# Cross-attention on one core: the K projection by seven 64x64 products per 2x2 step in place of eight

## What is computed

```python
Q = x @ W_Q      # x: 1024 x 128, W_Q: 128 x 1024, 16 heads of 64
K = ctx @ W_K    # ctx: 6404 x 128
V = ctx @ W_V
scores = Q K^T / 8                 # per head: 1024 x 6404
attn = softmax(scores, axis=-1)
out = (attn @ V, heads side by side) @ W_O + x
return (out - mean(out)) / sqrt(var(out) + 1e-5)   # per row
```

## Time and profile before

| | |
|---|---|
| median of 3 runs | 1600.99 us |
| the profiled execution | 1601.11 us |
| its span in the trace | 1599.3 us |
| TensorE matmuls busy | 1590.5 us (99%) |
| VectorE busy | 1314.6 us (82%) |
| ScalarE busy | 835.4 us (52%) |
| GpSimd busy | 64.2 us (4%) |
| odd pass, even pass | 91.0 us, 104.0 us |

### The profile page before, as it was taken

How to read it: one execution, slowest core, us unless ns; L and a number is a source line. 1 busy time by engine, 2 the same in 40 slices (tenths; PEclk the granted TensorE clock), 3 DMA queues, 4 the chain that set the end, 5 groups by cost and what they waited for, 6 DMA issues and landing times.

```text
span 1599.3 us, 39500 instructions
## 1 busy us (share of the span) xinstructions
PE 1590.5 (99%) x17484; PEld 1073.0 (67%) x17484; DVE 1314.6 (82%) x1229; ACT 835.4 (52%) x828; POOL 64.2 (4%) x41
## 2 busy tenths in 40 slices
PE   9999999999999999999999999999999999999998
PEld 4576677766777667766677666776677766777435
DVE  7788788887888788887798878988789887888877
ACT  4445554555545555456544565445654455544653
POOL 0001000010000001000010000000000000000100
PEclk9999999999999999999999999999999999999999
DMA  4000000000000000000000000000000000000000
GB/s 162 3 2 9 1 2 9 2 10 1 10 2 1 10 1 10 2 1 9 1 10 2 2 9 2 10 2 2 9 1 10 2 9 2 1 10 2 9 2 15
DMA packets 13006, 14.26 MB, mean 9 GB/s; under 512 B 4784, under 2 KB 8624, under 8 KB 12832
## 3 DMA queue, kind: packets, MB, share of 16 engines
q1 hardware_dynamic: 12544, 11.36, 2.3%
q10 hardware_dynamic: 288, 0.33, 0.1%
HBM read 10.60 MB, written 0.59 MB: 7 GB/s over the span
## 4 chain that ended last, share of the span: by engine, by line
PE 98%; DVE 1%; ACT 0%; issue 0%; DVEq 0%; ACTq 0%
PE o_ps L484 44%; PE s_ps L467 42%; PE w_ps L549 6%; PE w_ps L532 5%; PE s_ps L616 0%; DVE inv_sum L943 0%; DVE y L976 0%; DVE stats L963 0%; PE w_ps L564 0%; DVE y L959 0%; PE w_ps L607 0%; DVE inv_sum L809 0%; DVE sums L835 0%; DVE limits L985 0%; DVE k_all L809 0%
## 5 line engine op out<-in xcount | busy, mean ns | idle before, releaser
L728 ACT ACTIVATE probs<-s_ps 128x1024 f32<-128x1024 f32 x801 | 822.5, 1027 | 737.1 <-PE s_ps L467 737.1
L835 DVE TENSOR_TENSOR sums<-sums,probs 128x1024 f32<-128x1024 f32 x785 | 968.0, 1233 | 213.7 <-ACT probs L728 205.5
L484 PE MATMUL o_ps<-probs,v_all 64*64 64x512 f32 x6408 | 942.9, 589 | 0.0
L467 PE MATMUL s_ps<-q_sb,k_all 64*64 64x512 f32 x6408 | 942.8, 589 | 0.0
L467 PEld LDWEIGHTS s_ps<-q_sb,k_all 64*64 64x64 f32 x6408 | 447.8, 133 | 238.9 <-issue 39.0
L484 PEld LDWEIGHTS o_ps<-probs,v_all 64*64 64x64 f32 x6408 | 424.8, 133 | 204.9 <-issue 33.6
L532 PEld LDWEIGHTS w_ps<-wv_sb,ctx_all 64*64 64x64 f32 x3176 | 122.4, 132 | 30.6 <-issue 1.7
L809 DVE TENSOR_REDUCE k_all<-w_ps 128x512 f32<-128x1024 f32 (+2 forms) x104 | 122.8, 1181 | 16.0 <-PE w_ps L549 14.9
L809 DVE TENSOR_REDUCE v_all<-w_ps 128x512 f32<-128x1024 f32 (+2 forms) x103 | 121.8, 1182 | 15.8 <-PE w_ps L532 15.7
L532 PE MATMUL w_ps<-wv_sb,ctx_all 64*64 64x128 f32 x3176 | 120.0, 269 | 0.1
L549 PE MATMUL w_ps<-ctx_all,wk_sb 64*64 64x512 f32 (+2 forms) x832 | 119.3, 573 | 0.0
(11 more groups left out here) (85 smaller groups left out, 119.5 us busy)
## 6 DMA issues: line engine op xcount, KB each, us to landing
inv_sum<-inv_dram SPq DMA_DIRECT2D x30, 128.0 KB, 2.9
ctx_all<-in_ctxT SPq DMA_DIRECT2D x11, 256.0 KB, 5.1
quad_rows<-quad_sums SPq DMA_DIRECT2D x60, 4.0 KB, 1.8
x_sb<-in_x SPq DMA_DIRECT2D x1, 512.0 KB, 10.1
wo_sb<-in_wo SPq DMA_DIRECT2D x1, 512.0 KB, 11.3
left_rows<-p_left SPq DMA_DIRECT2D x30, 8.0 KB
inv_left<-inv_dram SPq DMA_DIRECT2D x30, 8.0 KB
wq_sb<-in_wq SPq DMA_DIRECT2D x1, 448.0 KB, 6.4
```

Source lines behind the costliest of these rows:

```text
L467: last = nc.tensor.matmul(s_ps[part(half), u % 2, head * QH:(head + 1) * QH], k_all[part(head), c * P + half * DH:c * P + (half + 1) * DH] ...
L484: last = nc.tensor.matmul(o_ps[part(head), rows, :], v_all[part(rows), c, part(head)], probs[part(rows), u % RING, head * QH:(head + 1) * QH],
L728: nc.scalar.activation(probs[:, u % RING, :], s_ps[:, u % 2, :], ACT.Exp, scale=SCALE).then_inc(probs_ready, 1)
L835: nc.vector.tensor_tensor(out=sums[0:rows, t % 2, :], in0=sums[0:rows, t % 2, :], in1=probs[0:rows, u % RING, :], op=ALU.add).then_inc(sum ...
```

## The change

From the second pair on, K of each of the 12 full blocks is made by Strassen's scheme: W_K of the pair is a 2x2 matrix of 64x64 blocks, the context of 256 keys a 2x2 matrix of 64x128 blocks, and seven products of sums and differences of blocks replace eight. A block of 512 keys is two such steps, so 14 matmuls of 128 columns instead of 16 times 128 columns. Four of the seven contract in one row half (`one`) and three in the other (`two`), and `one` alternates with the block's number.

- **TensorE**: the work splits in a first part "r" (`seven_first`, 8 matmuls, two in each quarter) and a second part "k" (`seven_second`, 6 matmuls: two in each quarter of row half `one`, one in each of `two`). r stands at steps 0, 4, 8, ..., k at 2, 6, 10, ... and v at 3, 7, 11, ...; in the odd passes r, k, v stand at 38, 40, 41 and 42, 44, 45.
- **ScalarE** copies three of the products to the other 64 partitions, and one as it is, between r and k (`cross`, three instructions).
- **GpSimd** takes two differences of them (`sum_crossed`, two instructions of 128 columns), and makes the sums and differences of W_K once per pair (`form_weights`, 8 instructions).
- **VectorE** finishes K with three instructions (`take_seven`) where there was one.
- The sums of context blocks (`c_forms`, 128x768 floats a block) don't fit in SBUF. GpSimd makes them once, during the first two passes, a block at a time (`form_keys`, four instructions): SyncE reads the context with its halves exchanged, GpSimd adds, SyncE writes 393 KB to `forms_dram`. Later SyncE reads them back, two slots ahead of r.
- GpSimd's `add_halves` and `norm` of the first pass now stand behind all of `form_keys`, and SyncE's `quad_rows` of the first pass behind all of the writing and behind the first reads.
- The keys of a block lie in `k_all` in another order, which `product` undoes by its choice of V's chunk.

```diff
--- before.py
+++ after.py
+    NEXT_STEPS = (0, 36, 38, 40, 41, 42, 44, 45)
+    NORM_STEP, W_FORMS_STEP = 13, 20
+    LEFT_BEHIND = 7
...
+    def by_seven(pair, b):
+        return pair > 0 and 0 <= b < FULL_BLOCKS
...
+            if by_seven(pair, at // 4 + 2) and at % 4 in (0, 2):
+                return ("rk"[at % 4 // 2], pair, at // 4 + 2)
             if at >= 0 and at % 4 == 0 and at // 4 + 2 < BLOCKS:
                 return ("k", pair, at // 4 + 2)
-            if at >= 2 and at % 4 == 2 and at // 4 + 2 < BLOCKS:
+            if at >= 2 and at % 4 == (2 if t == 0 else 3) and at // 4 + 2 < BLOCKS:
                 return ("v", pair, at // 4 + 2)
-        elif pair + 1 < PAIRS and c in (0, 36, 38, 40, 42, 44):
-            n = (0, 36, 38, 40, 42, 44).index(c)
-            return (("q", "q", "k", "v", "k", "v")[n], pair + 1, (0, 1, 0, 0, 1, 1)[n])
+        elif pair + 1 < PAIRS and c in NEXT_STEPS:
+            n = NEXT_STEPS.index(c)
+            return ("qqrkvrkv"[n], pair + 1, (0, 1, 0, 0, 0, 1, 1, 1)[n])
...
+            READY[found] = READY[before] + (before[0] != "r") if len(COUNT) > 1 else 1
+            before = found
...
+        c_forms = sb("c_forms", [P, 2, FORM_COLS])
+        w_forms = sb("w_forms", [P, 6, 2 * DH])
+        crossed = sb("crossed", [P, BLOCK, P])
+        forms_dram = nc.dram_tensor("forms_dram", [FULL_BLOCKS, P, FORM_COLS], F32, kind="Internal").ap()
...
+            def load_turned(b):
+                if b > 0:
+                    sp.wait_ge(c_forms_ready, b)
+                if b > 1:
+                    sp.wait_ge(c_forms_stored[b % 2], 16 * (b // 2))
+                for half in range(2):
+                    sp.dma_start(crossed[part(half), :, :].rearrange("p n k -> p (n k)"),
+                                 ctxT[part(1 - half), b * BK:(b + 1) * BK]).then_inc(turned_ctx_loaded, 16)
...
+            def store_forms(b):
+                sp.wait_ge(c_forms_ready, b + 1)
+                sp.dma_start(forms_dram[b, :, :], c_forms[:, b % 2, :]).then_inc(c_forms_stored[b % 2], 16)
+            def load_forms(pair, b):
+                n = seven_index(pair, b)
+                if n < 2:
+                    for slot in range(2):
+                        sp.wait_ge(c_forms_stored[slot], 16 * (FULL_BLOCKS // 2))
+                else:
+                    sp.wait_ge(work_done, COUNT["k", pair - (b < 2), (b - 2) % FULL_BLOCKS])
+                sp.dma_start(c_forms[:, n % 2, :], forms_dram[b, :, :]).then_inc(c_forms_loaded[n % 2], 16)
+            def load_turned_w(pair):
+                if pair > 1:
+                    sp.wait_ge(work_done, COUNT["k", pair - 1, FULL_BLOCKS - 1])
+                for half in range(2):
+                    sp.dma_start(w_forms[part(half), 0, :], w_k[part(1 - half), pair * P:(pair + 1) * P]
+                                 ).then_inc(turned_w_loaded, 16)
+            load_turned(0)
+            for b in range(FULL_BLOCKS):
+                if b == LEFT_BEHIND:
+                    load_left(0)
+                store_forms(b)
+                if b + 1 < FULL_BLOCKS:
+                    load_turned(b + 1)
             sp.wait_ge(left_zeroed, 2)
             for t in range(PASSES - 1):
+                pair, h = (t + 1) // 2, (t + 1) % 2
+                if h == 1 and pair + 1 < PAIRS:
+                    load_turned_w(pair + 1)
+                    for b in range(2):
+                        load_forms(pair + 1, b)
+                if h == 0:
+                    for b in range(2, 5):
+                        load_forms(pair, b)
                 sp.wait_ge(quad_sums_ready, t + 1)
                 for i in range(QUADS):
...
+                if h == 0:
+                    load_forms(pair, 5)
                 sp.wait_ge(inv_lines_ready, t + 1)
...
+                if h == 0:
+                    for b in range(6, FULL_BLOCKS):
+                        load_forms(pair, b)
...
+            def form_keys(b):
+                one, two = part(b % 2), part(1 - b % 2)
...
+                nc.gpsimd.tensor_tensor(out=forms[one, :, 0:2, :], in0=as_is[one, :, :, :], in1=turned_ctx[one, :, :, :],
+                                        op=ALU.add).then_inc(c_form_step, 1)
+                pool.wait_ge(c_form_step, 3 * b + 1)
+                nc.gpsimd.tensor_tensor(out=forms[two, :, 0, :], in0=as_is[two, :, 1, :], in1=turned_ctx[two, :, 0, :],
+                                        op=ALU.subtract).then_inc(c_form_step, 1)
+                pool.wait_ge(c_form_step, 3 * b + 2)
+                nc.gpsimd.tensor_tensor(out=forms[two, :, 1, :], in0=as_is[two, :, 0, :], in1=as_is[two, :, 1, :],
+                                        op=ALU.add).then_inc(c_form_step, 1)
+                pool.wait_ge(c_form_step, 3 * b + 3)
+                nc.gpsimd.tensor_tensor(out=forms[two, :, 2, :], in0=turned_ctx[two, :, 0, :], in1=turned_ctx[two, :, 1, :],
+                                        op=ALU.add).then_inc(c_forms_ready, 1)
...
+            def sum_crossed(pair, b):
+                n = seven_index(pair, b)
+                pool.wait_ge(crossed_ready, 3 * (n + 1))
+                m4, m3, m1 = (1, 2, 3) if b % 2 == 0 else (2, 3, 1)
+                nc.gpsimd.tensor_tensor(out=crossed[:, m4, :], in0=crossed[:, m4, :], in1=crossed[:, 0, :],
+                                        op=ALU.subtract).then_inc(crossed_summed, 1)
+                pool.wait_ge(crossed_summed, 2 * n + 1)
+                nc.gpsimd.tensor_tensor(out=crossed[:, 0, :], in0=crossed[:, m3, :], in1=crossed[:, m1, :],
+                                        op=ALU.subtract).then_inc(crossed_summed, 1)
...
+            for b in range(FULL_BLOCKS):
+                form_keys(b)
+            pool.wait_ge(c_forms_ready, FULL_BLOCKS)
+            for t in range(1, PASSES):
+                for c in range(FULL_CHUNKS):
+                    if c == 0:
+                        add_halves(t - 1)
+                    found = work_at(t, c)
+                    if found is not None and found[0] == "r":
+                        sum_crossed(found[1], found[2])
+                    if c == NORM_STEP:
+                        norm(t - 1)
+                    if c == W_FORMS_STEP and t % 2 == 1 and t // 2 + 1 < PAIRS:
+                        form_weights(t // 2 + 1)
...
+            def seven_first(found):
+                _, pair, b = found
+                n, one, two = seven_index(pair, b), b % 2, 1 - b % 2
+                main, extra, m1 = seven_slots(b)
+                pe.wait_ge(work_ready, READY[found] - 1)
+                pe.wait_ge(w_forms_ready, pair)
+                pe.wait_ge(c_forms_loaded[n % 2], 16 * (n // 2 + 1))
+                for i in range(2):
+                    g = part(1 - i)
+                    nc.tensor.matmul(main[g, 0, 1, :], w_form(one, 0, 1 - i), form(one, pair, b, i, 0), start=True, stop=True)
+                    nc.tensor.matmul(extra[g, 0, :], w_form(two, 5, i), form(two, pair, b, i, 2), start=True, stop=True)
+                for i in range(2):
+                    h = part(i)
+                    at = pair * P + i * DH
+                    nc.tensor.matmul(main[h, 1, 1, :], wk_sb[part(one), at:at + DH], form(one, pair, b, i, 1),
+                                     start=True, stop=True)
+                    last = nc.tensor.matmul(m1[h, :], w_form(two, 3, i), form(two, pair, b, i, 0), start=True, stop=True)
+                last.then_inc(work_done, 1)
...
+            def seven_second(found):
+                _, pair, b = found
+                n, one, two = seven_index(pair, b), b % 2, 1 - b % 2
+                main, extra, _ = seven_slots(b)
+                pe.wait_ge(crossed_ready, 3 * (n + 1))
+                for i in range(2):
+                    nc.tensor.matmul(extra[part(i), 1, :], w_form(two, 4, i), form(two, pair, b, i, 1), start=True, stop=True)
+                for i in range(2):
+                    at = b * BK + 2 * i * P
+                    nc.tensor.matmul(main[part(i), 1, 0, :], w_form(one, 1, i), form(one, pair, b, i, 2), start=True, stop=True)
+                    last = nc.tensor.matmul(main[part(1 - i), 0, 0, :], w_form(one, 2, 1 - i), ctx_all[part(one), at:at + P],
+                                            start=True, stop=True)
+                last.then_inc(work_done, 1)
...
+            def cross(pair, b):
+                n = seven_index(pair, b)
+                act.wait_ge(work_done, COUNT["r", pair, b])
...
+                apart = w_ps[:, :, :].rearrange("p r (s k) -> p (r s) k", k=P)[:, 1 + b % 2 * 2:6 + b % 2 * 2:2, :]
+                for half in range(2):
+                    nc.scalar.activation(crossed[part(1 - half), 1:4, :], apart[part(half), :, :],
+                                         ACT.Copy).then_inc(crossed_ready, 1)
+                nc.scalar.activation(crossed[:, 0, :], seven_slots(b)[2], ACT.Copy).then_inc(crossed_ready, 1)
...
+            def take_seven(found):
+                _, pair, b = found
```

(13 more changed lines are left out.)

119 lines of the change are left out of this document (94 added, 25 removed).

## The result

The changed kernel takes 1650.4 us (median of four runs, 1649.6 to 1651.2), the kernel before beside it 1600.8: a ratio of 1.031, with a 95% interval of 1.029 to 1.033. The change costs 49.6 us. The forecast was 1632, its range 1608 to 1658. The direction was right and so was most of the mechanism; the size was 18 us short.

What follows compares the result with a forecast made beforehand. The prediction took TensorE, with a matmul in flight 99% of the span, as the bound. It added 1.3 + 3.9 + 19.5 + 6.2 + 0.3 = 31.2 us to 1601.1 us, giving 1632 us, range 1608 to 1658.

Steps and rivals of the forecast that it cites:

- Rival 1: Rounds of sums at the start much longer, 12.5 us each, giving a 28 us stall and 1654 us; chance 0.12.
- Rival 2: TensorE's small matmuls don't keep up, 2 x 0.11 us a block, 18 us in all, 1650 us; chance 0.07.
- ordinary waits (passes 1.3, V's wait 3.9): TensorE: 84 blocks 0.015 us dearer each without a lead, and V waiting 0.05 us for K in 77 blocks.
- steps 2, 40 and 9: Other VectorE work queued there makes TensorE wait 0.86, 0.83 and 1.1 us, 7 times each, +19.5 us.
- stall in the second pass: `quad_rows` lands at 152.8 behind twelve rounds of sums, so TensorE stalls until 156.2, +6.2 us.
- first pass: GpSimd's hold on the port it shares with VectorE, +0.3 us.
- walk through VectorE's queue: From K's second part: VectorE free at 0.81, `take_seven` ends at 2.15, V starts at 2.20 instead of 2.16.
- ScalarE's three copies ... I cost them at nothing: About 1.3 us a block in the 3.4 us between r and k, costed at nothing.
- upper bound of 0.3 us: Most that V's ordinary wait could be, if `cross` or GpSimd's shared port pushes VectorE's addition back.
- No lead gain: TensorE's lighter quarters could run ahead, gaining at most 8.2 us, but V's wait for K prevents it; none taken.
- rival 4: Matmuls in program order, VectorE just in time: nothing saved, little lost, 1602 to 1612 us; chance 0.08.
- Rival 3: Faster, 1593 us: `take_seven` ends before 1.95 us, the lead survives and the start's sums are hidden; chance 0.08.

Runs made afterwards that it cites:

- e_moves_3: `e_moves_2` with the read of block 5's sums put ahead of the wait for `quad_sums` on SyncE's queue; 1624.1 us, ratio 1.015.
- e_moves: The changed kernel with the once-a-pass steps (turn, folding, inversion, norm, left keys' addition, `add_halves`) moved to other places; 1630.4 us, ratio 1.018.
- e_setup: The changed kernel with the first pass's inverses ahead of the last rounds of sums on SyncE's queue; 1641.0 us, ratio 1.025.
- e_two_copies: The changed kernel without the third of ScalarE's three copies (K wrong in the blocks by seven); 1651.6 us, ratio 1.032.
- e_all_3: The changed kernel with `e_spread`, `e_moves_3` and `e_setup` together, and K of the last keys at step 41 instead of 40 in even passes; 1596.4 us, ratio 0.9971.
- e_short_take: The changed kernel without the last of the three VectorE instructions in K's taking (K wrong in the blocks by seven); 1627.7 us, ratio 1.017.
- e_all: The changed kernel with K's second part and VectorE's takings of K and V earlier, plus `e_moves_2` and `e_setup`; 1619.7 us, ratio 1.012.
- e_moves_2: `e_moves` with the folding at step 8 instead of 5; 1632.4 us, ratio 1.019.
- e_spread: The changed kernel with TensorE's r and V of the blocks by seven each behind the product of their step; 1623.3 us, ratio 1.013.

## Why the prediction was right, and where it was short

The measured time lies in the range, but 4 us outside the forecast's own part of it (1618 to 1646). It fell where the range had been widened for rivals 1 and 2, and what happened was neither of them. So that the range held owes something to luck. The forecast passes were 106.5 and 92.0 us, the measured ones 108.4 and 92.35. The terms of the sum, forecast and measured (us):

| step of the prediction | forecast | measured | shown by |
|---|---|---|---|
| ordinary waits (passes 1.3, V's wait 3.9) | 5.2 | 17.4 (7 x 2.48) | what `e_moves_3` has left over before |
| steps 2, 40 and 9 | 19.5 | 18.9 | `e_moves_3`: 22.5, less the next line |
| step 2, V (not forecast) | 0 | 3.6 (7 x 0.51) | `e_moves` |
| stall in the second pass | 6.2 | 9.0 to 9.3 | `e_setup` |
| first pass | 0.3 | 0.9 | windows |

**The walk through VectorE's queue was right in its parts.** The taking's 1.34 us is exact. The three once-a-pass waits, 0.86, 0.83 and 1.1 forecast, are 0.76 (`r` at step 4), 0.95 (`r` at step 42) and 1.04 (V at step 11). That they don't hang on hundredths was right too: all of them vanish when the steps are moved, and come back elsewhere when they are put too close.

**The ordinary wait was mis-sized, and it turned out to be nearly the largest term.** The step that failed is "ScalarE's three copies ... I cost them at nothing". The forecast had it in its upper bound of 0.3 us. They end 0.1 us too late, and the exponential, the addition and the taking shift by 0.08, which `e_two_copies` shows (a block of 8.72 in place of 8.80, and this exponential 1.19 us behind its scores in place of 1.27). What is left to 0.20 is near the forecast 0.065, plus 0.05 us by which `r` comes later behind V (2.64 us, 2.59 where V doesn't wait, as in `e_all_3`). Such a small number stands 84 times in the sum; a wait that is worked out as the difference of 2.20 and 2.16 can't be known to better than 0.1. It could shrink by 0.05 at most and grow by 0.25, so its likeliest value should have lain further from the lower bound.

**The wait at step 2 was missed.** The prediction gave GpSimd's port a price in the first pass alone, and named it besides only in the upper bound of the ordinary wait. The even passes had `add_halves` before too, but beside a taking from PSUM, which it didn't disturb. The diff moves nothing on GpSimd's queue ahead of `add_halves`; it is VectorE's order beside it that changed, and I read VectorE's queue only against TensorE.

**The stall was 3 us short.** A round takes 10.77 us, not 10.5 ((149.29 - 30.77) / 11), the first reads landed 1.4 us later, and `quad_rows` at 156.5 in place of 152.8: 3.7 us later. The stall took 1.1 of them, since TensorE's next scores were due at 152.66 (150.94 + 1.72) and not at 150.0: one step more than reckoned, and a first pass 0.9 us longer. From `quad_rows` to the next scores it was 3.43 us, the forecast's 3.4. The other 1.75 are the clock, of which the text said that no row shows it and took nothing. A bound from the lower level, the step behind the stall at half speed, could have been put beside it.

**No lead gain, as forecast, and for the reason given.** In the changed kernel the lighter quarters do run ahead: behind the second part of 294.52 the first two of the product's matmuls start at 294.73 and the other two at 294.97. V's wait takes that back. The prediction's condition was that a taking which ends before 1.95 us keeps the lead. In `e_short_take` it ends at 1.90 in every other block and blocks are 8.54 us; in `e_all_3` they are 8.51 (two in 17.01, from the K of 263.16 to that of 280.17). TensorE's timeline there, at the end of a second part:

```profile
289.00 0.60 PE L680 MATMUL o_ps<-probs,v_all 64*64 64x512 f32 x2
289.03 0.27 PE L785 MATMUL w_ps<-ctx_all,w_forms 64*64 64x128 f32 x1
...
289.13 1.02 PE L680 MATMUL o_ps<-probs,v_all 64*64 64x512 f32 x6
```

Two of the product's matmuls begin ahead of the last of K, which stands earlier in the program, as at the earlier trace rows. (The trace has two records for each matmul, so the x6 there are the records of all four, and not "six matmuls", as the prediction reads them; its 0.16 us stands.) The block's gain of 0.09 us is nearly the 0.10 that the prediction has for a full eighth of 0.87 us. The Trainium skill (TensorE: Matmul & The Clock Gate, Part 3, what overlaps and what doesn't) has matmuls start strictly in program order; with 64 by 64 tiles the rows disagree, and rival 4, which rested on that rule, has lost its ground by the block of 8.51 us. With no quarter ahead of another that block could not have been under 8.60.

**The rivals.** Rival 1 (longer rounds) had the right neighbour but not the size: 0.27 us a round. Rival 2 (small matmuls don't keep up) gave exactly the measured time, 1650, and is wrong: in `e_all_3` the steps with `r` take 0.43 us over 1.72, which is two matmuls a quarter at the rate of V's (four in 0.87), and those with the second part 0.30 and 0.35 in turn. There is no 0.11 us left over in either. A time that fits says nothing for a mechanism. Rival 3 (faster) was right on what would have to be true, and it became true by another order, not in this kernel.

What stays open: some 7 of the 27 us of `e_all`, the 0.3 us by which an even pass of `e_all_3` gained less than ten times 0.09, and how much of the first pass's 1.2 us is GpSimd's hold on VectorE.

## What to carry to other kernels

On a full TensorE an edit that saves columns is worth its columns only if nobody waits behind it; here a gain of at most 8 us stood against 50 us of waits, most of them on an engine whose share of busy time fell. Walk the queue of the engine that takes the result, with the once-a-pass steps in it, and add up the slack at each place rather than the load. And when a step is moved, list what is queued behind its signals on every other queue: two of these experiments lost 7 and 13 us to one DMA that stood behind a wait.

## What the runs showed of the hardware that I had not expected

- **Who comes first on the shared port decides who pays.** `norm` started 0.07 us behind an addition and took 2.28 us, the addition 1.22; started 0.12 us ahead of one it took 1.27, and the addition 2.24. Seven such turns a run are 6.5 us on TensorE, and an edit elsewhere (one copy fewer on ScalarE) turned them round. The taking of K from PSUM beside `add_halves` was not slowed (1.22 us). The Trainium skill (VectorE: DVE Perf Modes, Two Vector instructions with no wait between them) has a VectorE instruction with two SBUF tensor inputs read the second through an interface shared with GpSimd; the rows agree, 2.04 and 2.24 us for such additions, and show besides that the one that comes second is held for about as long as the other still runs.
- **The granted clock falls with a single stall, and not only a long one:** TensorE stood still for 6.98 us, to 159.97, then the clock was 0.50 (1.2 GHz) for 3.5 us at full work and 1.00 again, for 1.75 us of loss. In `e_all` a standstill of 2.57 us was enough (0.50 for the 3.4 us behind it), while one of 2.04 us in the same run and one of 2.17 in `e_moves_2` left it at 1.00, as did all the waits of the changed kernel's other passes, at most 1.0 us each.
- **A wait of TensorE costs a little more than itself.** Where V waited, `r` came 2.64 us behind it, where it did not, 2.59. `e_spread` has both in one pass: the V of 242.06 starts 0.06 us after K's taking has ended, and `r` comes 2.64 behind it; the V of 276.78 starts 0.39 after, and `r` comes 2.59 behind.
